# Chunked linear attention: scores and keys by separate TensorE passes instead of one merged product

## The chip, the cores and the metric

The kernel runs on one core of a Trainium2 chip. A core has five engines with queues of their own: TensorE (matmuls, PE in the profile, its weight loads PEld), VectorE (DVE), ScalarE (ACT), GpSimd (POOL) and SyncE (SP, which only issues DMAs here). They are joined by semaphores. The metric is the time on the device of one execution, in microseconds, as the median of several runs.

## The reference

An AdaLN block on x of 8 x 2048 x 256: a layer norm with modulation, gated linear attention, a gate and a residual, then a second layer norm with a mixture of 8 experts (two chosen for each token), a gate and a residual. The change touches the attention alone:

```
q = elu(x @ Wq) + 1        # 16 heads of 64
k = elu(x @ Wk) + 1
v = x @ Wv
a = sigmoid(x @ Wa + ba + 2.0)            # one decay for each head and token
def step(carry, inp):                     # along the 2048 tokens
    S = at[..., None, None] * S + kt[..., :, None] * vt[..., None, :]
    z = at[..., None] * z + kt
    num = einsum('bhk,bhkv->bhv', qt, S)
    den = einsum('bhk,bhk->bh', qt, z) + eps
    return (S, z), num / den[..., None]
out = out @ Wo
```

## The kernel before

The tokens go through in 32 groups of 512 (GT), and the recurrence along them is cut into chunks of 64 (CK), eight to a group (NCK). The heads are taken two at a time, 8 pairs (PAIRS) to a group. A **step** is one pair of one group, so there are 256 steps, with three more at the start in which only the early stages run. All engines walk through the same steps (`attention_steps`), the first and last groups unrolled, the ones between in a loop. The stages of a pair are spread over the steps: in step u TensorE makes K and Q for the pair three ahead (`project`, L594 to L596), applies the state to the queries of the pair one ahead (L741), makes the chunks' own state updates for the pair two ahead (L755), adds the masked scores times V for the pair one ahead (L766), transposes the output of the present pair (L782), does one or two large jobs of a fixed table (V, output projection, decays, the next group's transposes), and last comes the block that is changed (L803 to L822), for the pair three ahead. It waits for K and Q of its pair (`k_ready`, `q_ready`), for the readers of its PSUM tile (`kd_ready`, `p_ready`) and, except in the first step of a group, for `oT_hi_ready`, since L782 writes the same bank.

**The changed block.** K and Q of a pair lie transposed in SBUF (`qk_sb`): head 0 on partitions 0 to 63, head 1 on 64 to 127, 512 tokens along. The block makes two things from them. The scores of each chunk, S = K Q^T of 64 x 64 (tile `S`), which VectorE multiplies by a decay mask into `p_sb` (L980). And the keys turned to have tokens on the partitions (tile `KTR`), which ScalarE copies with a decay factor into `kd_sb` (L554, eight copies), the weights' partner in L755. Both are in `bank_scores`, one PSUM bank for each head, KTR in the first half of a bank and S in the second. `place(hd, ch)` says on which half of the partitions and in which column block t a chunk lands: head 0 in order, head 1 one chunk further back, so that its chunk 0 lands last, beside chunk 7.

Before, the two are one product. An identity of 64 x 64 (`eye`) lies in `qk_sb` ahead of Q, and the moving operand is a view with a stride that takes the identity and one chunk of Q, 2 x 64 columns (`eye_q`); the stationary operand is that chunk of K. So 16 products of 64 x 64 weights and 128 columns make both. Consecutive products lie on different quarters of TensorE's array of 128 x 128: the head gives the rows, `place` the columns. A product of fp32 operands is two records in the profile. GpSimd copies the identity to its place at the start (L413), and TensorE waits for it once (`eye_ready`).

The profile writes a product as out<-moving,stationary, with the weights' rows*columns, then the output's partitions x columns. A weight load has a record of its own (PEld).

Of the kernel before, what the change touches and what calls it, by code (L numbers as in the profile page):

```python
# [39 lines left out]
CH = 128  # L40
CK = 64
SLICE = CH // 4
NCH = 4
GT = CH * NCH
NCK = GT // CK
# [10 lines left out]
def after(eng, sem, count):  # L56

    if isinstance(count, int) and count <= 0:
        return
    eng.wait_ge(sem, count)  # L60


def exists(T):

    return not isinstance(T, int) or 0 <= T < NG
# [7 lines left out]
def unit(T, u, ahead):  # L73

    Tn, p = (T, u + ahead) if u + ahead < PAIRS else (T + 1, u + ahead - PAIRS)
    return Tn, p, Tn * PAIRS + p
# [49 lines left out]
def adaln_block(nc, x, Wq, Wk, Wv, Wo, Wa, ba, gate_W, gate_b, expert_W, expert_b, c, wmod, out):  # L126
    tokens = x.rearrange("b (g c p) d -> (b g) p c d", p=CH, c=NCH)
    out_tokens = out.rearrange("b (g c p) d -> (b g) p c d", p=CH, c=NCH)
    x1_dram = nc.dram_tensor("x1_dram", [NG, CH, NCH, D], F32, kind="Internal").ap()
    rows_dram = nc.dram_tensor("rows_dram", [2, 2, PAIRS, 2, GT], F32, kind="Internal").ap()  # L130
    gates_dram = nc.dram_tensor("gates_dram", [2, BATCH, D], F32, kind="Internal").ap()

    with ExitStack() as keep:
        mod = keep.enter_context(nc.sbuf_tensor("mod", [128, 4, KT, BATCH], F32))
        ident = keep.enter_context(nc.sbuf_tensor("ident", [128, 128], F32))
        def psum(name, shape):
            return keep.enter_context(nc.psum_tensor(name, shape, F32))

        single = [psum(f"bank{i}", [128, 512]) for i in range(2)]
        bank = single + [psum(name, [128, 2, 512]) for name in ("bank_scores", "bank_dense", "bank_nums")]  # L140
        attention_phase(nc, tokens, Wq, Wk, Wv, Wo, Wa, ba, c, wmod, x1_dram, gates_dram, rows_dram, mod, ident, bank)
        expert_phase(nc, x1_dram, gates_dram, gate_W, gate_b, expert_W, expert_b, out_tokens, mod, ident, bank)


def attention_phase(nc, tokens, Wq, Wk, Wv, Wo, Wa, ba, c, wmod, x1_dram, gates_dram, rows_dram, mod, ident, bank):
    with ExitStack() as ctx:
        def sb(name, shape, dt=F32):
            return ctx.enter_context(nc.sbuf_tensor(name, shape, dt))

        def sem(name):  # L150
            return ctx.enter_context(nc.semaphore(name))
# [11 lines left out]
        eye8 = sb("eye8", [128, NCK, CK])  # L163
# [7 lines left out]
        x_res = sb("x_res", [128, NCH, D])  # L171
# [18 lines left out]
        oT_lo = sb("oT_lo", [128, PT, GT], F32R)  # L190
        oT32 = sb("oT32", [128, GT])

        qk_sb = sb("qk_sb", [128, CK + 2 * GT])
        eye, q_sb, k_sb = qk_sb[:, 0:CK], qk_sb[:, CK:CK + GT], qk_sb[:, CK + GT:CK + 2 * GT]
        qs_sb = sb("qs_sb", [128, 2, GT])
        decay = sb("decay", [128, 2, NCH, CK])
        p_sb = sb("p_sb", [128, 2, 2, NCH, CK])
# [12 lines left out]
        Q, K, SCORES, EXTRA, NUM = bank[0][:, :], bank[1][:, :], *bank[2:]  # L210
        U_ODD, U_EVEN = EXTRA[:, 0, :], EXTRA[:, 1, :]
        KTR, S = SCORES[:, :, 0:GT // 2], SCORES[:, :, GT // 2:GT]
        HT = [K, SCORES[:, 1, :]]
        MODS, GATES = [NUM[:, 1, :], SCORES[:, 0, :]], NUM[:, 0, :]
        KTR_S = SCORES[:, :, :].rearrange("p h (x t i) -> p h x t i", x=2, t=NCH)
        U = [(U_EVEN, U_ODD)[ch % 2][:, ch // 2 * VW:(ch // 2 + 1) * VW] for ch in range(NCK)]
        def o_bank(u):

# [6 lines left out]
        consts_ready = sem("consts_ready"); ones_ready = sem("ones_ready"); fills = sem("fills")  # L225
# [14 lines left out]
        decay_ready = sem("decay_ready"); qs_ready = sem("qs_ready")  # L240
        s_ps = sem("s_ps"); p_ready = sem("p_ready")
        kd_ready = sem("kd_ready")
        u_ps = sem("u_ps"); eye_ready = sem("eye_ready"); entry_cleared = sem("entry_cleared"); state_step = sem("state_step")
        inter_ps = sem("inter_ps"); num_ps = sem("num_ps"); den_step = sem("den_step"); o_ready = sem("o_ready")
        oT_ps = sem("oT_ps"); oT32_ready = sem("oT32_ready"); oT_hi_ready = sem("oT_hi_ready"); oT_lo_ready = sem("oT_lo_ready")

# [1 line left out]
        def wide(t, dims):  # L248
            return t.rearrange(f"p {dims} -> p ({dims})")

        v_flat = wide(v_sb[:, :, :, :], "c h v")
        p_flat = wide(p_sb[:, :, :, :, :], "a h t i")
        qk_flat, qs_flat, res_flat = qk_sb[:, CK:CK + 2 * GT], wide(qs_sb[:, :, :], "a n"), wide(x_res[:, :, :], "c d")
        wmod_part = [[p_flat[:, 0:3 * D], qk_flat[:, 0:3 * D]], [qs_flat[:, 0:3 * D], res_flat[:, 0:3 * D]]]
        W = KT * P_DIM
        WV, WK, WQ, WO0, WO1 = range(5)
# [17 lines left out]
        def place(hd, ch):  # L274

            m = (ch - hd) % NCK
            return m % 2, m // 2

        def v_col(p, hd):

            return p // 4 * 8 + hd * 4 + p % 4
# [99 lines left out]
        def _(pool):  # L381
            def reciprocal_deviation(T):
                pool.wait_ge(var_ready, T + 1)
                pool.tensor_tensor(rstd[:, :], var_eps[:, :], half_neg[:, :], ALU.pow).then_inc(rstd_ready, 1)
# [24 lines left out]
            for t, fill, pattern in ((eye8[:, :, :], 1.0, [[0, NCK], [-1, CK]]), (first[:, :], 1.0, [[-1, 1]]), (later[:, :], 0.0, [[-1, 1]])):  # L409
                pool.affine_select(out=t, in_=t, compare_op=ALU.not_equal, fill=fill, base=-CK, pattern=pattern,  # L410
                                   channel_multiplier=1).then_inc(consts_ready, 1)
            pool.wait_ge(consts_ready, 4)
            pool.tensor_copy(eye, eye8[:, 0, :]).then_inc(eye_ready, 1)  # L413
            reciprocal_deviation(0)
            ln_apply(0, range(NCH))

# [51 lines left out]
        def _(act):  # L468
# [3 lines left out]
            def split_weight(n):  # L472
                hi, _, raws = big_w[n]
                act.wait_ge(w_loaded[n], 16 * LOADS[n])
                for part, raw in kept(hi, raws):
                    ins = act.activation(part, raw, ACT.Copy)
                ins.then_inc(hi_split, 1)
# [39 lines left out]
            def step(T, place_in_batch, u):  # L517
                s = place_in_batch % 2
                n = T * PAIRS + u
                Ta, _, a = unit(T, u, 3)  # L520
                if exists(Ta):

# [39 lines left out]
        def _(pe):  # L562
# [3 lines left out]
            for kt in range(KT):  # L566
                mm = pe.transpose(K[:, kt * BATCH:(kt + 1) * BATCH], c_e[:, kt * 128:(kt + 1) * 128],
                                  ident[0:BATCH, 0:BATCH])
# [138 lines left out]
            def step(T, place_in_batch, u):  # L707
                s = place_in_batch % 2
                n = T * PAIRS + u
                Tc, pc, c = unit(T, u, 1)  # L710
                Tb, pb, b = unit(T, u, 2)
                Ta, pa, a = unit(T, u, 3)
                sa = s if u + 3 < PAIRS else 1 - s
                sc = s if u + 1 < PAIRS else 1 - s
                rows = [slice(i * CK, (i + 1) * CK) for i in range(2)]
# [15 lines left out]
                if exists(Tc):  # L731
# [5 lines left out]
                    for ch in range(NCK):  # L737
                        state = carry[:, sc, pc, :] if ch == 0 else s_mid[:, pc % 2, ch - 1, :]
                        query = slice(ch * CK, (ch + 1) * CK)
                        for hd in range(2):  # L740
                            mm = pe.matmul(NUM[rows[ch % 2], hd, ch // 2 * VW:(ch // 2 + 1) * VW], qs_sb[rows[hd], pc % 2, query],  # L741
                                           state[rows[hd], :], start=(ch < 2), stop=False)
                    mm.then_inc(inter_ps, 1)
                if exists(Tb):
# [7 lines left out]
                    for ch in range(NCK):  # L752
                        for hd in range(2):
                            half, t = place(hd, ch)
                            mm = pe.matmul(U[ch][rows[hd], :], kd_sb[rows[half], t, rows[hd]], v_sb[rows[half], t, v_col(pb, hd), :],  # L755
                                           start=True, stop=True)
                    mm.then_inc(u_ps, 1)
                if exists(Tc):
# [4 lines left out]
                    for ch in range(NCK):  # L763
                        for hd in range(2):
                            half, t = place(hd, ch)
                            mm = pe.matmul(NUM[rows[ch % 2], hd, ch // 2 * VW:(ch // 2 + 1) * VW], p_sb[rows[half], pc % 2, hd, t, :],  # L766
                                           v_sb[rows[half], t, v_col(pc, hd), :], start=False, stop=(ch >= NCK - 2))
# [32 lines left out]
                if exists(Ta):  # L800

                    if isinstance(Ta, int) and a == 0:
                        pe.wait_ge(mod_ready, 4)  # L803
                        pe.wait_ge(gates_step, 4)
                    pe.wait_ge(k_ready, a + 1)
                    pe.wait_ge(q_ready, a + 1)
                    after(pe, kd_ready, a)
                    after(pe, p_ready, a)
                    if u and exists(T):
                        pe.wait_ge(oT_hi_ready, n + 1)  # L810
                    if u == 0 and exists(T + 1):
                        pe.wait_ge(h32_ready, T * 2 + 4)
                    if isinstance(Ta, int) and a == 0:
                        pe.wait_ge(eye_ready, 1)
                    pe.sem_inc(inputs_seen)
                    for ch in range(NCK):
                        eye_q = qk_sb[:, 0:2 * (ch + 1) * CK].rearrange("p (x i) -> p x i", x=2)[:, :, 0:CK]
                        for hd in range(2):
                            half, t = place(hd, ch)
                            mm = pe.matmul(KTR_S[rows[half], hd, :, t, :], k_sb[rows[hd], ch * CK:(ch + 1) * CK], eye_q[rows[hd], :, :],  # L820
                                           start=True, stop=True)
                    mm.then_inc(s_ps, 1)  # L822

            attention_steps(pe, step)

        @block.vector
        def _(dve):
# [16 lines left out]
            def split_weight(n):  # L844
                hi, lo, raws = big_w[n]
                dve.wait_ge(hi_split, n + 1)
                for (low, raw), (high, _) in zip(kept(lo, raws), kept(hi, raws)):
                    ins = dve.tensor_tensor(low, raw, high.bitcast(F32), ALU.subtract)
                ins.then_inc(lo_split, 1)
# [618 lines left out]
```

## Time and profile before

| | us |
|---|---|
| median of 3 runs | 3352.62 |
| the runs | 3346.16, 3352.62, 3356.04 |
| the profiled execution | 3356.36 |
| its span, first to last instruction | 3354.6 |
| TensorE busy | 3235.5 (96%) |
| VectorE, ScalarE, GpSimd busy | 2455.1, 1812.7, 1437.3 |

The attention phase ends near 2500 us; after it the experts' phase runs to the end. The profile gives starts and durations of single instructions. On TensorE a product's duration reaches from its start to a modelled end, and products overlap, so that the distance from start to start tells what one costs in a row of them. A timeline row joins neighbours of one line: its second number is the time from the first one's start to the last one's end, x its count.

### The profile page before, as it was taken

What the parts mean: (1) busy time and instruction counts of PE and PEld (TensorE: products, weight loads), DVE (VectorE), ACT (ScalarE), POOL (GpSimd) and SP (SyncE); (2) the same over time, 40 slices, a digit from 0 to 9 for tenths busy, and PEclk for the clock granted to TensorE, in tenths of its full rate; (3) what the DMA queues carried; (4) which work ended last, traced back from release to release, by engine and by line L of the source; (5) the groups of instructions that cost most, each with busy time, mean ns of one, the idle gap of its engine ahead of it and who ended that gap; (6) DMA issues with size and microseconds to landing.
All of it is one profiled execution on the core that took longest, in us unless ns stands there. A gap on an engine that the chain in (4) does not pass through costs nothing. (4 is left out here: it accounts for less than half of the span.)

```text
span 3354.6 us, 129353 instructions
## 1 busy us (share of the span) xinstructions
PE 3235.5 (96%) x51114; PEld 2748.1 (82%) x51114; DVE 2455.1 (73%) x6681; ACT 1812.7 (54%) x4492; POOL 1437.3 (43%) x1117
## 2 busy tenths in 40 slices
PE   7999999999999999999999999999987999999999
PEld 5888888888888888888888888888875888878887
DVE  6777777777777776777777777777756788878786
ACT  5666666666666666666666666666642322222321
POOL 4444445545544444455455444444431222222222
PEclk9999999999999999999999999999997999999999
DMA  4222222222222222222222322222212111111110
GB/s 150 75 76 78 80 79 79 79 73 75 83 90 79 76 79 76 79 79 77 74 75 81 92 78 77 78 77 79 72 43 83 46 44 39 51 39 39 51 39 26
DMA packets 158613, 238.74 MB, mean 71 GB/s; under 512 B 30216, under 2 KB 82488, under 8 KB 157752
## 3 DMA queue, kind: packets, MB, share of 16 engines
q1 hardware_dynamic: 158008, 230.33, 21.9%
q8 instruction: 421, 6.90, 0.9%
q14 instruction: 184, 1.51, 0.1%
HBM read 194.58 MB, written 35.67 MB: 69 GB/s over the span
## 5 line engine op out<-in xcount | busy, mean ns | idle before, releaser
L447 POOL TENSOR_TENSOR qs_sb<-lam_bc,qk_sb 128x512 f32<-128x512 f32 x256 | 534.0, 2086 | 1081.5 <-DVE qk_sb L945 980.1
L554 ACT ACTIVATE kd_sb<-bank_scores,decay 128x64 f32<-128x64 f32 x2048 | 446.2, 329 | 288.5 <-PE bank_scores L820 278.8
L928 DVE SCALAR_TENSOR_TENSOR s_mid<-s_mid,lam_bc,bank_dense 128x65 f32<-128x65 f32 x1536 | 433.4, 282 | 55.1 <-DVE s_mid L928 0.3
L455 POOL TENSOR_TENSOR oT_lo<-oT,oT_hi 128x512 fp32r<-128x512 f32 x256 | 327.4, 1279 | 79.4 <-ACT oT_hi L531 79.1
L513 ACT ACTIVATE qk_sb<-bank 128x512 f32<-128x512 f32 x512 | 316.7, 619 | 54.0 <-PE bank L596 36.4
L1140 POOL TENSOR_TENSOR acc<-acc,gb 128x512 f32<-128x512 f32 x64 | 82.9, 1296 | 583.3 <-DVE acc L1312 559.8
L515 ACT ACTIVATE qk_sb<-qk_sb 128x512 f32<-128x512 f32 x512 | 323.3, 631 | 16.2
L980 DVE TENSOR_TENSOR p_sb<-bank_scores,decay 128x512 f32<-128x512 f32 x256 | 176.5, 689 | 206.7 <-ACT kd_sb L554 204.8
L594 PE MATMUL bank<-wv_hi,h_hi 128*128 128x256 f32 x1024 | 307.3, 300 | 7.1 <-DVE qk_sb L943 4.0
L951 DVE TENSOR_TENSOR_SCAN decay<-a_bc,eye 128x512 f32<-128x512 f32 x256 | 310.9, 1214 | 2.4 <-DMA a_bc<-rows_dram 2.4
L1312 DVE SCALAR_TENSOR_TENSOR acc<-bank,comb,acc 128x256 f32<-128x256 f32 x512 | 229.9, 475 | 107.5 <-ACT acc L1180 97.0
L820 PE MATMUL bank_scores<-qk_sb 64*64 64x128 f32 x8192 | 287.0, 276 | 8.6 <-ACT oT_hi L531 4.3
L689 PE MATMUL bank<-wo_hi,oT_hi 128*128 128x256 f32 x1024 | 290.9, 284 | 1.6 <-DVE xo L858 0.8
L595 PE MATMUL bank<-wv_lo,h_hi 128*128 128x256 f32 x1024 | 288.3, 282 | 0.7 <-issue 0.7
L596 PE MATMUL bank<-wv_hi,h_lo 128*128 128x256 f32 x1024 | 289.0, 282 | 0.0
L691 PE MATMUL bank<-wo_hi,oT_lo 128*128 128x256 f32 x1024 | 288.3, 282 | 0.0
L690 PE MATMUL bank<-wo_lo,oT_hi 128*128 128x256 f32 x1024 | 288.1, 281 | 0.0
L945 DVE SCALAR_TENSOR_TENSOR qk_sb<-bank,qk_sb 128x512 f32<-128x512 f32 x256 | 176.6, 690 | 127.0 <-ACT qk_sb L515 126.0
L820 PEld LDWEIGHTS bank_scores<-qk_sb 64*64 64x64 f32 x8192 | 227.2, 133 | 49.2 <-issue 35.3
L1312 DVE SCALAR_TENSOR_TENSOR acc<-bank_scores,comb,acc 128x256 f32<-128x256 f32 x512 | 231.1, 476 | 44.1 <-PE bank_scores L1226 42.9
L530 ACT ACTIVATE oT<-bank_scores 128x512 f32<-128x512 f32 x224 | 134.0, 598 | 218.5 <-PE bank_scores L782 217.1
L594 PE MATMUL bank<-h_hi,wk_hi 128*128 128x512 f32 x512 | 227.9, 445 | 14.1 <-ACT oT_hi L531 10.0
(198 smaller groups left out, 8605.5 us busy)
## 6 DMA issues: line engine op xcount, KB each, us to landing
a_bc<-rows_dram SPq DMA_DIRECT2D x512, 128.0 KB, 3.0
lam_bc<-rows_dram SPq DMA_DIRECT2D x512, 128.0 KB
x_in<-in_L_attn_x_dram SPq DMA_DIRECT2D x32, 512.0 KB, 5.6
x_res<-in_L_attn_x_dram SPq DMA_DIRECT2D x32, 512.0 KB, 4.0
x_dram<-x_res SPq DMA_DIRECT2D x32, 512.0 KB, 2.9
x<-x_dram SPq DMA_DIRECT2D x32, 512.0 KB, 3.3
out_dram<-x SPq DMA_DIRECT2D x32, 512.0 KB, 2.9
ew_raw<-in_L_ffn_expert_W_dram SPq DMA_DIRECT2D x8, 256.0 KB, 5.5
```

Source lines behind the costliest of these rows:

```text
L447: pool.tensor_tensor(qs_sb[:, na, :], lam_bc[na][:, :], q_sb, ALU.mult).then_inc(qs_ready, 1)
L455: pool.tensor_tensor(oT_lo[:, u, :], oT32[:, :], oT_hi[:, u, :].bitcast(F32), ALU.subtract).then_inc(oT_lo_ready, 1)
L513: act.activation(t, x[:, :], ACT.Relu, scale=-1.0).then_inc(x_neg, 1)
L515: act.activation(t, t, ACT.Exp, scale=-1.0).then_inc(x_exp, 1)
L554: ins = act.activation(kd_sb[:, t, hd * DH:(hd + 1) * DH], KTR[:, hd, t * CK:(t + 1) * CK], ACT.Copy, scale=decay[:, hd, t, CK - 1:CK])
L594: pe.matmul(dst, s_hi, m_hi, start=(n == 0), stop=False)
L596: mm = pe.matmul(dst, s_lo, m_hi, start=False, stop=(n == last))
L689: pe.matmul(dst, oT_hi[:, pt, tok], wo_hi[:, pt, :], start=(pt == 0 and i == 0), stop=False)
L820: mm = pe.matmul(KTR_S[rows[half], hd, :, t, :], k_sb[rows[hd], ch * CK:(ch + 1) * CK], eye_q[rows[hd], :, :], start=True, stop=True)
L928: dve.scalar_tensor_tensor(dst, src, lam_bc[nb][:, (ch + 1) * CK - 1:(ch + 1) * CK], U[ch], ALU.mult, ALU.add).then_inc(state_step, 1)
L951: dve.tensor_tensor_scan(decay[:, :, :, :].rearrange("p h t i -> p (h t i)"), a_bc[na][:, :], eye8[:, :, :].rearrange("p c i -> p (c i)"), ...
L1312: dve.scalar_tensor_tensor(a, y[:, (k // 2) * D:(k // 2 + 1) * D], comb[s % 2][:, 2 * pair + i, e:e + 1], a, ALU.mult, ALU.add).then_inc(y ...
```

## The change

The block makes scores and keys apart.

- Scores: 16 products as before, but with the 64 columns of Q alone.
- Keys: where two neighbouring chunks lie on the 128 partitions of one column block, one transpose takes 64 rows and 128 tokens and writes all 128 partitions. There are seven of them, four for head 0 and three for head 1. In head 1's last column block chunks 7 and 0 meet, which aren't neighbours; these two stay products with an identity of 64 x 64, taken from `ident`.
- The last of the seven transposes tells the readers that the block is done. The identity in `qk_sb`, its copy on GpSimd and the wait for it are gone.

```
-        qk_sb = sb("qk_sb", [128, CK + 2 * GT])
-        eye, q_sb, k_sb = qk_sb[:, 0:CK], qk_sb[:, CK:CK + GT], qk_sb[:, CK + GT:CK + 2 * GT]
+        qk_sb = sb("qk_sb", [128, 2 * GT])
+        q_sb, k_sb = qk_sb[:, 0:GT], qk_sb[:, GT:2 * GT]
...
-            pool.wait_ge(consts_ready, 4)
-            pool.tensor_copy(eye, eye8[:, 0, :]).then_inc(eye_ready, 1)
...
-                    if isinstance(Ta, int) and a == 0:
-                        pe.wait_ge(eye_ready, 1)
                     pe.sem_inc(inputs_seen)
                     for ch in range(NCK):
-                        eye_q = qk_sb[:, 0:2 * (ch + 1) * CK].rearrange("p (x i) -> p x i", x=2)[:, :, 0:CK]
+                        tok = slice(ch * CK, (ch + 1) * CK)
                         for hd in range(2):
                             half, t = place(hd, ch)
-                            mm = pe.matmul(KTR_S[rows[half], hd, :, t, :], k_sb[rows[hd], ch * CK:(ch + 1) * CK], eye_q[rows[hd], :, :],
-                                           start=True, stop=True)
+                            pe.matmul(S[rows[half], hd, t * CK:(t + 1) * CK], k_sb[rows[hd], tok], q_sb[rows[hd], tok], start=True, stop=True)
+                    for ch in (NCK - 1, 0):
+                        half, t = place(1, ch)
+                        pe.matmul(KTR[rows[half], 1, t * CK:(t + 1) * CK], k_sb[rows[1], ch * CK:(ch + 1) * CK], ident[rows[1], rows[1]],
+                                  start=True, stop=True)
+                    for t in range(NCH):
+                        for hd in range(2 if t < NCH - 1 else 1):
+                            mm = pe.transpose(KTR[:, hd, t * CK:(t + 1) * CK], k_sb[rows[hd], t * CH + hd * CK:(t + 1) * CH + hd * CK],
+                                              ident[rows[hd], rows[hd]])
                     mm.then_inc(s_ps, 1)
```

On TensorE's queue, in a step whose large job is V: before, the block stands between V's last product and K's projection for the next pair. A name in brackets is a semaphore that is waited for; "64x2x64" is an output of 64 partitions and twice 64 columns.

```order
L596 MATMUL bank<-wv_hi,h_lo 128x256
L820 MATMUL bank_scores<-qk_sb 64x2x64 [waits p_ready,kd_ready,k_ready,q_ready]
L820 MATMUL bank_scores<-qk_sb 64x2x64 x15
L594 MATMUL bank<-h_hi,wk_hi 128x512 [waits v_ready,h_lo_ready]
L595 MATMUL bank<-h_lo,wk_hi 128x512
```

The same place now:

```order
L593 MATMUL bank<-wv_hi,h_lo 128x256
L815 MATMUL bank_scores<-qk_sb 64x64 [waits p_ready,kd_ready,k_ready,q_ready]
L815 MATMUL bank_scores<-qk_sb 64x64 x15
L818 MATMUL bank_scores<-ident,qk_sb 64x64 x2
L822 MATMUL bank_scores<-ident,qk_sb 128x64 x7
L591 MATMUL bank<-h_hi,wk_hi 128x512 [waits v_ready,h_lo_ready]
L592 MATMUL bank<-h_lo,wk_hi 128x512
```

Sixteen products have become 25 instructions in three kinds; the waits ahead and behind are the same, and nothing else on the queue has moved (its lines are numbered two or three lower).

On GpSimd's queue at the start, before:

```order
L410 AFFINE_SELECT chunk_later<-chunk_later 128x1
L413 COPY qk_sb<-eye 128x64 [waits consts_ready]
L384 TENSOR_TENSOR rstd<-var_eps,half_neg 128x4 [waits var_ready]
```

and now:

```order
L409 AFFINE_SELECT chunk_later<-chunk_later 128x1
L383 TENSOR_TENSOR rstd<-var_eps,half_neg 128x4 [waits var_ready]
```

The copy is gone.

## Rows read from the trace of the kernel before

**Rows 1.** Page, engines; windows: stretch, us, busy (instructions) by engine, clock, DMA.

```profile
PE 3235.5 (96%) x51114; PEld 2748.1 (82%) x51114; DVE 2455.1 (73%) x6681; ACT 1812.7 (54%) x4492; POOL 1437.3 (43%) x1117
...
100.00:2480.00 2380.00, 2331.25 (x43897) 2009.55 (x43888) 1732.91 (x4287) 1531.97 (x3954) 1174.48 (x828) 1.00 0.26 78
```

**Rows 2.** TensorE's waits from 100 to 2480 us: us in total, times, longest.

```profile
PE bank L594 <- DVE lam_row L902: 13.6, 24, 0.8
PE bank L594 <- ACT oT_hi L531: 8.9, 31, 0.3
...
PE bank_scores L820 <- issue: 0.5, 3, 0.2
```

**Rows 3.** Products by shape: busy us, mean ns; the third from the view of L820.

```profile
L820 PE MATMUL bank_scores<-qk_sb 64*64 64x128 f32 x8192 | 287.0, 276 | 8.6 <-ACT oT_hi L531 4.3 <-issue 0.5 <-ACT h L493 0.2
L755 PE MATMUL bank_dense<-v_sb,kd_sb 64*64 64x65 f32 x8192 | 173.3, 221 | 0.0
...
L820 PE MATMUL bank_scores<-qk_sb x8192: 266/269/473, 44.1 to 2486.2; 64*64 64x128 f32 x200
```

**Rows 4.** Timeline around one block: start, us to the last end, count.

```profile
1503.47 1.10 PE L820 MATMUL bank_scores<-qk_sb 64*64 64x128 f32 x32
...
1504.51 0.19 PEld L594 LDWEIGHTS bank<-h_hi,wk_hi 128*128 128x128 f32 x1 [0.17 <-issue]
```

**Rows 5.** The same block in three short windows, ending 0.11 us apart.

```profile
1503.47 0.34 PE L820 MATMUL bank_scores<-qk_sb 64*64 64x128 f32 x4
...
1503.47 0.45 PE L820 MATMUL bank_scores<-qk_sb 64*64 64x128 f32 x8
...
1503.47 0.56 PE L820 MATMUL bank_scores<-qk_sb 64*64 64x128 f32 x12
```

**Rows 6.** Timeline of the three blocks with 65 columns.

```profile
1499.80 0.27 PE L741 MATMUL bank_nums<-carry,qs_sb 64*64 64x65 f32 x2
...
1500.32 0.67 PE L755 MATMUL bank_dense<-v_sb,kd_sb 64*64 64x65 f32 x32
...
1500.78 0.67 PE L766 MATMUL bank_nums<-v_sb,p_sb 64*64 64x65 f32 x32
```

**Rows 7.** The transposes behind them: load, then two, three, four in growing windows.

```profile
1501.38 0.42 PEld L782 LDWEIGHTS bank_scores<-ident,o_sb 128*128 128x128 f32 x4
...
1501.38 0.44 PE L782 MATMUL bank_scores<-ident,o_sb 128*128 128x128 f32 x2
...
1501.38 0.55 PE L782 MATMUL bank_scores<-ident,o_sb 128*128 128x128 f32 x3
...
1501.38 0.66 PE L782 MATMUL bank_scores<-ident,o_sb 128*128 128x128 f32 x4
...
1501.55 0.49 PE L782 MATMUL bank_scores<-ident,o_sb 128*128 128x128 f32 x3
```

**Rows 8.** Timeline, experts' phase: from 128x128 to 128x32.

```profile
2560.85 0.40 PE L1226 MATMUL bank<-ew_hi,h_lo 128*128 128x512 f32 x1
2561.17 0.63 PEld L1244 LDWEIGHTS bank_dense<-gw,h 128*32 128x32 f32 x64 [0.36 <-issue]
```

**Rows 9.** Timeline, experts' phase: from 128 rows to 72.

```profile
2628.33 0.40 PE L1226 MATMUL bank<-ew_hi,h_lo 128*128 128x512 f32 x1
...
2628.34 0.67 PEld L1263 LDWEIGHTS bank_nums<-eb,combT 72*128 72x128 f32 x4
```

**Rows 10.** Weight loads of transposes by shape: busy us, mean ns.

```profile
L782 PEld LDWEIGHTS bank_scores<-ident,o_sb 128*128 128x128 f32 x896 | 94.5, 141 | 18.9 <-issue 3.6
L656 PEld LDWEIGHTS bank<-ident,a_cols 128*80 128x80 f32 x128 | 14.0, 118 | 1.6 <-issue 1.6
```

**Rows 11.** Timeline of the block's readers, and TensorE's next use of the keys.

```profile
1504.68 1.74 ACT L554 ACTIVATE kd_sb<-bank_scores,decay 128x64 f32<-128x64 f32 x8 [0.60 <-PE bank_scores L820]
...
1506.53 0.69 DVE L980 TENSOR_TENSOR p_sb<-bank_scores,decay 128x512 f32<-128x512 f32 x1
...
1508.02 0.69 PE L755 MATMUL bank_dense<-v_sb,kd_sb 64*64 64x65 f32 x32
```

More of the change, by code:

```diff
@@ L214, in attention_phase @@
         MODS, GATES = [NUM[:, 1, :], SCORES[:, 0, :]], NUM[:, 0, :]
-        KTR_S = SCORES[:, :, :].rearrange("p h (x t i) -> p h x t i", x=2, t=NCH)
         U = [(U_EVEN, U_ODD)[ch % 2][:, ch // 2 * VW:(ch // 2 + 1) * VW] for ch in range(NCK)]
@@ L242, in attention_phase @@
         kd_ready = sem("kd_ready")
-        u_ps = sem("u_ps"); eye_ready = sem("eye_ready"); entry_cleared = sem("entry_cleared"); state_step = sem("state_step")
+        u_ps = sem("u_ps"); entry_cleared = sem("entry_cleared"); state_step = sem("state_step")
         inter_ps = sem("inter_ps"); num_ps = sem("num_ps"); den_step = sem("den_step"); o_ready = sem("o_ready")
@@ L252, in attention_phase @@
         p_flat = wide(p_sb[:, :, :, :, :], "a h t i")
-        qk_flat, qs_flat, res_flat = qk_sb[:, CK:CK + 2 * GT], wide(qs_sb[:, :, :], "a n"), wide(x_res[:, :, :], "c d")
+        qk_flat, qs_flat, res_flat = qk_sb[:, 0:2 * GT], wide(qs_sb[:, :, :], "a n"), wide(x_res[:, :, :], "c d")
         wmod_part = [[p_flat[:, 0:3 * D], qk_flat[:, 0:3 * D]], [qs_flat[:, 0:3 * D], res_flat[:, 0:3 * D]]]
```

## The prediction

> **What bounds the kernel now.** Read the page's table of engines and the windows first [rows 1]: TensorE's matmuls are busy 3235.5 of 3354.6 us, and in the stretch from 100 to 2480 us, the attention phase, 2331.25 of 2380 us, at a granted clock of 1.00, which is the 2.4 GHz level. Busy time alone proves little, since the ends of matmuls are modelled, so read next what TensorE waited for in that stretch [rows 2]: 11 kinds of wait, from 13.6 us in 24 times down to 0.5, in 2380 us. No other engine holds it up. In that phase the time is the sum of what TensorE's queue takes, and what the change adds to or takes from that queue goes into the end nearly whole. The block that it rewrites (L820) runs once for each of 256 pairs of heads: 8192 matmul records are 32 a block, two to each of 16 products [rows 3]. It is nowhere after 2486 us, so the expert phase stays as it is.
>
> **How TensorE's queue is priced.** The durations in the grouped view overlap (276 ns each, but 35 ns of busy time for one), so I price by starts. One block of L820 [rows 4]: its first product starts at 1503.47, the next weight load (for K's projection, L594) at 1504.51. **The block takes 1.04 us.** Three windows that end 0.11 us apart show what it is made of [rows 5]: four products of 64x64, one on each quarter of the array, run together, and each four more lengthen the run from 0.34 to 0.45 to 0.56 us. So a round of four passes of 128 columns is 0.11 us; eight rounds are 0.88, the first has 0.02 more for a load that nothing hides, and 0.14 is left between the end of the last round (1504.37) and the load at 1504.51.
>
> The same with 65 columns [rows 6]: L741 starts at 1499.80, L755 at 1500.32, L766 at 1500.78. A block of 32 passes is 0.46 us, or 0.0575 a round, and L741, which like L820 comes behind products on the whole array, takes 0.52.
>
> Every change of the shape in which the array is cut costs a pause: the next weight load isn't done beside the last products. Behind L766 (64x64, the last round ends at 1500.78 + 8 x 0.0575 = 1501.24) the load of L782 (128x128) starts at 1501.38, 0.14 later [rows 6, 7]. Behind L1226 (128x128, started at 2560.85; a follower of its shape would come 0.23 behind, at 2561.08) the load of L1244 (128x32) starts 0.09 later [rows 8]. Behind a same-shaped product the load starts with the product before it (L1226 to L1263, 72 rows in a 128-row array, 0.01 us behind its start) [rows 9]. The new first weights then cost about 0.06 that nothing hides: L782's load at 1501.38, its second transpose at 1501.55, one round of 0.11 less [rows 7].
>
> **The change, part by part**, for one block.
> - Scores alone: 16 products of 64 columns in place of 128. The nearest row is L741's 0.52 for 65 columns behind whole-array products [rows 6]; with one column less, 0.51.
> - Two key products by the identity (the chunks that wrap round), 64x64, two passes each, both on the lower 64 rows and on different columns, so they run as a pair: two rounds of 0.0575, **0.115**. Same shape as the scores, so no pause.
> - Pause from 64x64 to 64 rows x 128 columns. No row shows this pair of shapes. Rows 6 to 8 bound it at 0.09 and 0.14 if a pause comes; rows 9 stand for none. I take 0.10, since at the end of a pair the last product starts nearly with the first, while four quarters start up to 0.05 apart. With 0.06 for the first weights: **0.16**.
> - Seven transposes, one record each, as L782's four are four records [rows 7]. L782 takes 0.11 each (0.44, 0.55, 0.66 us for two, three and four) with 128 moving columns and the whole array. The new ones move 64 columns. What sets the 0.11, the load of the weights or the moving columns? A transpose's load goes from 118 to 141 ns for 80 and 128 columns, about 0.48 ns a column, so it can run at 0.06 for 128; matmuls go from 221 to 276 ns for 65 and 128 columns, 0.87 ns a column, which is the 0.11 [rows 3, 10]. So the moving side binds and 64 columns should take 0.0575. Head 0 uses the upper 64 rows, head 1 the lower, with different banks; rows 5 show upper and lower halves at work together. Then four rounds do it: 4 x 0.0575 = **0.23**. One after the other it is 7 x 0.0575 = 0.40.
> - Pause at the end, to K's projection: 0.14 before, 0.10 now, since a single tile is last. **0.10**.
>
> Sum: 0.51 + 0.115 + 0.16 + 0.23 + 0.10 = 1.115 us against 1.04. **Each block takes 0.075 us more; 256 blocks, 19 us.** With both pauses at 0.09 it is 0.055 (14 us), with both at 0.14 0.155 (40 us).
>
> In other words: halving the scores' columns gives 0.52 - 0.11 x 8 = 0.42 back (0.88 to 0.46), and moving the keys by transposes costs 0.115 + 0.23 plus the extra pause of 0.16, which is more.
>
> The rest costs nothing. The copy of the identity on GpSimd goes from among its first instructions; TensorE's first block starts only at 44 us [rows 3]. The copies of the keys on ScalarE (L554) wait for the last product of the block, start at 1504.68 and take 1.74 us, to 1506.42; TensorE wants them at L755 at 1508.02 [rows 11]. 1.6 us of cover hide a start that is 0.1 later; were the cover gone, the same 0.1 would be added in each block. VectorE's masking (L980) follows them at 1506.53 and is wanted later still. The queue of waits on TensorE is as before but for one wait at the start. Against this some steps have waits that take up a later start (13.6 and 8.9 us over 55 steps [rows 2]); at 0.075 each they hide at most 4 us, which I leave out.
>
> Here a rule of the Trainium skill speaks against the change. By its page "TensorEngine Tiling (Array Packing)", Tiling Modes, Key Properties, another tiling mode drains TensorE where another tile of the same mode doesn't, and the page lists 64x128 and 64x64 as two modes. Rows 6 to 9 agree for other pairs of modes; without the drain the block would be 0.955, by the rule about 1.115. By its page "Perfetto Trace Analysis", Transposes, a logical transpose should be done as one and not as a product; the trace agrees that a transpose is one record and a product two [rows 3, 7], and the sum here goes the other way all the same.
>
> **The rivals.**
> - **One after the other** (slower still): the transposes of the two halves don't overlap. For it: all of them write all 128 partitions, and no row shows two tiles of 128 columns at once. Against: rows 5. Seven rounds in place of four: +0.17, so 0.245 a block, +63 us.
> - **A round of transposes stays at 0.11**, because the load or the mode binds and not the moving columns: 4 x 0.11 = 0.44, +0.21 more, so 0.285 a block, +73 us. Against it the slopes of rows 3 and 10. One after the other as well (7 x 0.11 = 0.77) it would be +157 us, the far bound, which I hold for very unlikely.
> - **No pause between the shapes** (the other side, faster): the array goes from quarters to halves as it goes from 128 to 72 rows in rows 9, because the columns of a half are only two quarters side by side. Then 0.16 goes and the block is 0.955, -0.085, -22 us. It decides at 0.085: where pause and first weights together cost less than that, the change gains. For it: no row has this pair. Against: L1226 to L1244 keeps all rows and cuts only columns, and pauses [rows 8].
> - **No pause, but one after the other**: 0.955 + 0.17 = 1.125, +22 us, as good as my forecast in time.
>
> **How the numbers follow.** Own sum 0.60; one after the other 0.18; 0.11 a round 0.07; no pause 0.12; no pause and in turn 0.03. The profiled execution took 3356.36 us; with 19 us it is 3375. It lies 4 us over the median of 3352.62, so against the median I forecast **3372 us**. The other cases against the median: 3416, 3426, 3331, 3375. The range leaves out "no pause" (0.12) and the far bound: from 3356, which is the low end of my sum less the 4 us of waits and the spread of the runs (3346 to 3356), to 3428. A measurement of this kernel can tell about 0.3%, 10 us, from no change. Faster by more: 0.12 of the no-pause case. Within: the low edge of my sum, 0.08. Slower: 0.80.
>
> **What would show it.** In the profile after: the start of the scores to the load of K's projection should be 1.1 us for 1.04; the 16 products 0.51; a gap of some 0.1 us before the first transpose's load; transposes in pairs of nearly the same start, 0.0575 apart. Transposes each 0.0575 apart mean one after the other; 0.11 apart, the load or mode binds; a first transpose load that starts with the last key product means no pause. ScalarE's wait for the block (278.8 us) should grow a little and cost nothing. Wrong would be: starts of other blocks that move too, a granted clock under 1.00 in the attention phase (transposes in place of products), or waits of TensorE that weren't there.

## The result

The changed kernel takes **3375.79 us** in the median of 4 runs (3375.30 to 3379.93), the kernel before 3353.09 (3346.16 to 3356.04). The ratio is 1.0074, with a 95% interval of 1.0062 to 1.0086 (the two medians alone give 1.0068): it is slower, by 22.7 us, under 1%. The profiled executions differ by 19.6 us in their spans, 3374.2 against 3354.6.

The page and the windows of the changed kernel, as [rows 1]:

```profile
span 3374.2 us, 134983 instructions
...
PE 3262.4 (97%) x53930; PEld 2785.5 (83%) x53930; DVE 2455.4 (73%) x6681; ACT 1814.8 (54%) x4492; POOL 1437.3 (43%) x1116
...
100.00:2500.00 2400.00, 2356.81 (x46646) 2044.85 (x46647) 1734.68 (x4290) 1534.48 (x3953) 1175.52 (x828) 1.00 0.25 78
```

TensorE has 2816 more matmul records, 11 for each of 256 blocks, and as many more loads. The other engines are as before, and the clock in the attention phase is again 1.00, so no part of the loss is the clock's. One block, the counterpart of [rows 4], in the timeline:

```profile
1517.30 0.69 PE L815 MATMUL bank_scores<-qk_sb 64*64 64x64 f32 x32
...
1517.82 0.29 PE L818 MATMUL bank_scores<-ident,qk_sb 64*64 64x64 f32 x4
1518.04 0.32 PEld L822 LDWEIGHTS bank_scores<-ident,qk_sb 64*128 64x128 f32 x7
1518.04 0.46 PE L822 MATMUL bank_scores<-ident,qk_sb 64*128 64x64 f32 x7
1518.43 0.19 PEld L591 LDWEIGHTS bank<-h_hi,wk_hi 128*128 128x128 f32 x1
```

L815 are the scores, L818 the two key products, L822 the transposes. From the first score to the load of K's projection it is 1.13 us where it was 1.04: 0.52 for the scores, 0.22 from the first key product to the first transpose's load, 0.39 from there to the end. The same block in growing windows, as [rows 5] and [rows 7]:

```profile
1518.04 0.28 PE L822 MATMUL bank_scores<-ident,qk_sb 64*128 64x64 f32 x2
1518.04 0.34 PE L822 MATMUL bank_scores<-ident,qk_sb 64*128 64x64 f32 x4
1518.04 0.40 PE L822 MATMUL bank_scores<-ident,qk_sb 64*128 64x64 f32 x6
```

Two more transposes lengthen it by 0.06 us: they run in pairs. Over all 256 blocks the median is 1.130 us against 1.033, by the starts in the trace to the nanosecond; that is 0.097 more. TensorE's waits, as [rows 2]:

```profile
PE bank L591 <- DVE lam_row L904: 11.8, 24, 0.8
PE bank_nums L763 <- issue: 8.9, 8, 1.6
PE bank L591 <- ACT oT_hi L528: 5.7, 29, 0.2
```

Those for `lam_row` and `oT_hi` fell by 1.8 and 3.2 us. A longer block takes up what TensorE would have waited in the few steps where another engine sets the time. So 256 x 0.097 - 5.0 = 19.8 us, against 19.6 measured between the spans. The rows named "issue" add up to 19.3 us here and 17.5 before, 1.8 more, which leaves the sum 2 us too high. Each kernel has one trace, and the kernel before varies by 12 us in 15 runs (3347.9 to 3359.7), so that no such sum can be trusted to less than some us.

### The profile page after: what moved, and what is told of

Read it like the earlier page. It is cut to its first block and busy times, and to the rows that moved or that the text cites. A ratio compares the mean times of both kernels' runs of the same rounds, so it can differ in the third digit from the quotient of the medians.

```text
span 3374.2 us, 134983 instructions
## 1 busy us (share of the span) xinstructions
PE 3262.4 (97%) x53930; PEld 2785.5 (83%) x53930; DVE 2455.4 (73%) x6681; ACT 1814.8 (54%) x4492; POOL 1437.3 (43%) x1116
## 5 line engine op out<-in xcount | busy, mean ns | idle before, releaser
L551 ACT ACTIVATE kd_sb<-bank_scores,decay 128x64 f32<-128x64 f32 x2048 | 446.2, 328 | 304.9 <-PE bank_scores L822 294.6
L947 DVE SCALAR_TENSOR_TENSOR qk_sb<-bank,qk_sb 128x512 f32<-128x512 f32 x256 | 176.7, 690 | 132.3 <-ACT qk_sb L512 130.6
L945 DVE SCALAR_TENSOR_TENSOR qk_sb<-bank,qk_sb 128x512 f32<-128x512 f32 x256 | 175.9, 687 | 61.7 <-ACT qk_sb L512 59.9
L591 PE MATMUL bank<-h_hi,wq_hi 128*128 128x512 f32 x512 | 204.4, 399 | 13.7 <-DVE lam_row L904 13.5
```

Source lines behind the costliest of these rows:

```text
L551: ins = act.activation(kd_sb[:, t, hd * DH:(hd + 1) * DH], KTR[:, hd, t * CK:(t + 1) * CK], ACT.Copy, scale=decay[:, hd, t, CK - 1:CK])
L591: pe.matmul(dst, s_hi, m_hi, start=(n == 0), stop=False)
```

## The experiments

My theory had three parts: TensorE's queue sets the time; a round of work that fills the array costs what its longer side (load or moving columns) takes; and each change between shapes of the array costs a pause and a first load that nothing hides. Each experiment changes one of these. Lengths of blocks are medians over 256, from the first product's start to the load of K's projection; times are medians, ratios are to the kernel before on the same chip. The experiments used three chips, on which the kernel before took 3353.1, 3350.1 (products of 128 columns, head by head, wrap products twice) and 3352.4 us (output in halves). In the experiments the lengths of the blocks came within 0.012 us of their forecasts but for head by head; four of the times missed theirs by 12 to 45 us, and that of head by head by 30. Where I add up below what makes a time, the waits and "issue" are read from the trace of that same run: it is an account afterwards, not a forecast.

| kernel | block, us | forecast | time, us | ratio (95%) |
|---|---|---|---|---|
| before | 1.033 | | 3353.1 | |
| changed | 1.130 | 1.115 | 3375.8 | 1.0074 (1.0062 to 1.0086) |
| all products | 1.090 | 1.09 | 3378.6 | 1.0078 (1.0063 to 1.0094) |
| products of 128 columns | 1.772 | 1.76 | 3489.6 | 1.0414 (1.0383 to 1.0444) |
| transposes split | 1.272 | 1.28 | 3405.1 | 1.0158 (1.0143 to 1.0174) |
| head by head | 1.130 | 1.25 to 1.31 | 3375.2 | 1.0073 (1.0050 to 1.0096) |
| wrap products twice | 1.246 | 1.246 | 3390.3 | 1.0117 (1.0088 to 1.0146) |
| transposes first | 1.127 | 1.13 | 3373.6 | 1.0062 (1.0046 to 1.0077) |
| ring of keys | 1.016 | 1.012 | 3349.6 | 0.9991 (0.9982 to 1.0000) |
| output in halves, with the ring | | | 3360.0 | 1.0022 (1.0012 to 1.0031) |

### One pause more: the transposes split

```
+                    for t in range(2):
+                        for hd in range(2 if t < NCH - 1 else 1):
+                            mm = pe.transpose(KTR[:, hd, t * CK:(t + 1) * CK], ...)
                     for ch in range(NCK):            # the scores
...
-                    for t in range(NCH):
+                    for t in range(2, NCH):
```

> The same work as in the changed kernel, with four of the seven transposes ahead of the scores and three behind, so that the array changes shape once more in each block. My theory: one more pause of 0.09 us and one more first load of 0.06, 0.15 a block, 38 us less what some steps hide, so 3376 + 35 = 3411. Rival, a change of shape costs nothing of its own and the gap ahead of the transposes is something else (the end of the block's queue, a wait): as the changed kernel, 3376.

```profile
1530.67 0.34 PE L813 MATMUL bank_scores<-ident,qk_sb 64*128 64x64 f32 x4
1530.93 0.56 PEld L819 LDWEIGHTS bank_scores<-qk_sb 64*64 64x64 f32 x32
...
1531.68 0.33 PE L826 MATMUL bank_scores<-ident,qk_sb 64*128 64x64 f32 x3
1531.94 0.19 PEld L591 LDWEIGHTS bank<-h_hi,wk_hi 128*128 128x128 f32 x1
```

In the timeline the four transposes (L813) start at 1530.67, and the load of the scores comes at 1530.93. By the starts in the trace (medians over all blocks) that load is 0.151 us behind the start of the last of the four; a round of 0.06 of that is work, and 0.09 is pause. With some 0.05 for the first load that nothing hides (in the changed kernel the second pair of transposes starts 0.112 behind the first, the next ones 0.06) it is about the 0.142 that the block grew. The block is 1.272 us against 1.130, by the same instructions in another order. The time is 3405.1, 29 us more, 6 less than expected: the waits for `oT_hi` and `lam_row` had 17.5 us to give in the changed kernel, and here only 5.7 are left. With 4.3 more at "issue" (idle time that is told of below) the sum is 256 x 0.142 - 11.8 + 4.3 = 28.9 us; the spans of the profiled executions, from which the waits come, differ by 24.4, the medians by 29.3. The pause has its price, and the rival without one is out.

### The place doesn't matter: all transposes first

```
+                    for t in range(NCH): ... mm = pe.transpose(...)     # all seven, ahead of the scores
                     for ch in range(NCK): ...
                     for ch in (NCK - 1, 0): ...
-                    for t in range(NCH): ... mm = pe.transpose(...)
```

> The same work as in the changed kernel, all seven transposes ahead of the scores, the two products by the identity last. As many changes of shape as in the changed kernel, in other places. My theory: 3376, within 5 us. Rival, the place matters (the first transposes wait for less, or the readers get the block's end at another time): off by more than 10 us.

3373.57 us, 2 us from the changed kernel; its own runs (3371.8 to 3379.8) take in the changed kernel's median. As many changes of shape, the same time; that they stand at the end and the readers wait for the last of them plays no part that can be seen.

### No third shape: all products

```
-                    for ch in (NCK - 1, 0):
+                    for ch in range(NCK):
+                        for hd in range(2):
+                            half, t = place(hd, ch)
+                            mm = pe.matmul(KTR[rows[half], hd, t * CK:(t + 1) * CK], k_sb[rows[hd], ch * CK:(ch + 1) * CK],
+                                           ident[rows[hd], rows[hd]], start=True, stop=True)
...
-                    for t in range(NCH): ... mm = pe.transpose(...)
```

> The scores as in the changed kernel, the keys as 16 products of 64x64 by the identity; no transposes and no third shape of the array. My theory (TensorE's queue is priced by rounds of 0.058 us and by pauses between shapes): 16 rounds of four passes, 0.93 us, with 0.05 at the start and 0.15 at the end make a block of 1.09 us against 1.033 before and 1.129 in the changed kernel, so about 14 us slower than before, 3366. Rival 1, the whole loss of the changed kernel comes from the transposes and their pause: without them as before, 3353. Rival 2, the loss comes from the number of instructions: here 64 passes and loads each where the changed kernel has 43, so slower than it, over 3385.

The block came out at 1.090 us, as forecast, 0.057 more than before: 16 rounds of 0.058 cost more than 8 of 0.109, so merging alone was worth that much. The time didn't: 3378.6, where 3366 was expected, and the same as the changed kernel's although its blocks are 0.04 shorter. Neither rival explains it. What does is the rows "issue" of the waits (stretch 100 to 2530):

```profile
PE bank_nums L763 <- issue: 9.4, 11, 1.5
PE bank L591 <- issue: 8.7, 6, 5.0
PE bank L591 <- ACT oT_hi L528: 7.2, 31, 0.2
```

"issue" is idle time in which TensorE waited for nothing that the profile shows. Added over its rows it is 17.5 us before, 19.3 in the changed kernel, 26.5 here. By the sum: 256 x 0.057 = 14.6, 4.0 less by the waits for `lam_row` and `oT_hi`, 9.0 more by "issue", 19.6 us; the spans differ by 21.0. Such a stop can stand in the midst of a block and come back at the same place of the program. Here is one in both passes of the loop, 936.4 us apart:

```profile
708.23 0.44 PE L819 MATMUL bank_scores<-ident,qk_sb 64*64 64x64 f32 x16
708.91 0.46 PE L819 MATMUL bank_scores<-ident,qk_sb 64*64 64x64 f32 x16 [0.24 <-issue]
...
1644.64 0.44 PE L819 MATMUL bank_scores<-ident,qk_sb 64*64 64x64 f32 x16
1645.33 0.46 PE L819 MATMUL bank_scores<-ident,qk_sb 64*64 64x64 f32 x16 [0.24 <-issue]
```

Sixteen records, 0.24 us of idle array, sixteen records, in the same step of the loop's body both times (the two blocks are 96 blocks apart). No semaphore stands between these records, and the place in the instruction stream plays a part. It isn't all of it: compared record by record over the two passes, 10 places of this kernel have a stop in both (neighbouring starts of one line over 0.1 us beyond the distance that 95% of that line keep to) and 10 in one pass alone; before there are 3 and 4, in the changed kernel 4 and 4. This kernel has the longest stream of the ten (485 instruction transfers on the page for 421 before). That the supply of instructions is the cause is argued, not shown; no run here changes it by itself.

### What sets a round: products of 128 columns

```
-                            mm = pe.transpose(KTR[:, hd, t * CK:(t + 1) * CK], k_sb[rows[hd], ...], ident[rows[hd], rows[hd]])
+                            mm = pe.matmul(KTR[:, hd, t * CK:(t + 1) * CK], k_sb[rows[hd], ...], ident[rows[hd], rows[hd]],
+                                           start=True, stop=True)
```

> The seven transposes as plain products of the same 64 rows and 128 columns by the identity, two passes each. My theory: a load of 128 columns for a plain fp32 pass takes twice that of a transpose, 0.11 us, so the load and not the 64 moving columns sets a round; eight rounds of 0.11, 0.88 us, in place of four of 0.06: 0.63 a block, 160 us, so about 3535. Rival, the moving columns set the round here too: eight rounds of 0.06, 0.24 more, 3435.

```profile
1584.13 1.10 PE L822 MATMUL bank_scores<-ident,qk_sb 64*128 64x64 f32 x14
1585.16 0.19 PEld L591 LDWEIGHTS bank<-h_hi,wk_hi 128*128 128x128 f32 x1
...
L822 PEld LDWEIGHTS bank_scores<-ident,qk_sb 64*128 64x128 f32 x3584 | 246.8, 187 | 17.3
```

Fourteen passes take 1.03 us where seven transposes take 0.39. The moving columns are the same 64; the load has changed, from 138 ns (the changed kernel's L822) to 187 ns on average. A plain product may differ from a transpose in more than that, so compare the scores too: they are plain passes with 64 moving columns, their loads of 64 columns take 134 ns, and a round takes 0.058. Both ways the load is about 0.05 us longer here and the round as well. So the load sets the round here, at 0.11, and the block is 1.772, 0.64 more, as expected. The time is 3489.6, and not 3535: of 164 us more in the blocks the spans show 112. The waits that could give way did: those for `lam_row` and `oT_hi` (17.5 us) are gone, and of "issue" 5.4 are left of 19.3. That is 31 us, and 21 are left. Most of them are in the way of counting, since idle time is counted from modelled ends, behind the real ones. From start to start, the blocks grew by 154.5 us in all and not by 164 (those of the changed kernel hold more waits and stops), 15.8 went ahead of Q's projection, where the waits for `lam_row` were, and 9.2 inside the products of L763; some 17 are left, in pieces of 3 us and less.

### Who runs with whom: head by head

```
-                    for t in range(NCH):
-                        for hd in range(2 if t < NCH - 1 else 1):
+                    for hd in range(2):
+                        for t in range(NCH - hd):
```

> The same seven transposes, the four of head 0 first and then the three of head 1, so that neighbours in the queue are on the same rows. My theory: the pairs of the changed kernel work at the same time because they are neighbours on different rows; in this order only the last of head 0 and the first of head 1 can, so six rounds of 0.0615 in place of four, 0.12 to 0.18 more, 31 to 46 us, 3405 to 3422. Rival, TensorE finds the other rows' transposes further down its queue: as the changed kernel, 3376.

```profile
1514.71 0.28 PE L822 MATMUL bank_scores<-ident,qk_sb 64*128 64x64 f32 x2
1514.71 0.35 PE L822 MATMUL bank_scores<-ident,qk_sb 64*128 64x64 f32 x4
1514.71 0.41 PE L822 MATMUL bank_scores<-ident,qk_sb 64*128 64x64 f32 x6
```

My theory fell. With head 0's four ahead of head 1's three the growing windows read as in the changed kernel, two more for each 0.06, and the block is 1.130. TensorE takes the other rows' transposes from further down its queue. The trace shows it: the last of the seven in the queue (head 1's third) is the one whose record carries the update of `s_ps`, and in 255 of 256 blocks it starts sixth, with another transpose starting behind it; in the changed kernel it starts last in all. That also rules out that any two neighbours pair, whatever their rows. That they run in pairs stands; that they must be neighbours for it doesn't. Whether the update could come before the one behind has ended, no run here shows.

### The price of the two key products: done twice

```
-                    for ch in (NCK - 1, 0):
+                    for ch in (NCK - 1, 0, NCK - 1, 0):
```

> The changed kernel with its two products by the identity done twice. My theory: two rounds of 0.058 more, 0.117 a block, 29 us less what some steps hide, 3403. Rival, the two overlap with what is around them and their price is near nothing: 3376 to 3383.

The block is 1.246, 0.116 more, as forecast for two rounds. The time is 3390.3, 14.5 us more than the changed kernel's and not 27. The blocks add 256 x 0.116 = 29.7; the waits for `lam_row` fell from 11.8 to 8.0 and those for `oT_hi` from 5.7 to none, 9.5; "issue" fell from 19.3 to 13.2. That leaves 14.1, and the spans differ by 15.1. The rival without a price for them is out by the block.

### Without them: the ring of keys

```
-        qk_sb = sb("qk_sb", [128, 2 * GT])
+        qk_sb = sb("qk_sb", [128, 2 * GT + CK])
+        k_ring = qk_sb[:, GT:2 * GT + CK]
...
+                    pool.wait_ge(k_ready, a + 1)
+                    pool.tensor_copy(k_ring[:, GT:GT + CK], k_sb[:, 0:CK]).then_inc(ring_ready, 1)
...
-                    for ch in (NCK - 1, 0): ...                            # the two key products
                     for t in range(NCH):
-                        for hd in range(2 if t < NCH - 1 else 1):
+                        for hd in range(2):                                # from k_ring in place of k_sb
```

> The two products by the identity are gone: the keys get 64 more columns, which GpSimd fills with a copy of chunk 0, so that chunks 7 and 0 of head 1 are neighbours and an eighth transpose takes them, in the round in which head 0's last was alone. My theory: two rounds of 0.058 go, the block is 1.129 - 0.117 = 1.012 us against 1.033 before; 3376 - 29 = 3347, some 5 us faster than before. Rival, GpSimd's copy comes late in some steps and TensorE waits for it: slower than the changed kernel in those steps, 3360 or more, with a new wait for GpSimd in the list.

```profile
1495.90 0.69 PE L819 MATMUL bank_scores<-qk_sb 64*64 64x64 f32 x32
1496.52 0.32 PEld L822 LDWEIGHTS bank_scores<-ident,qk_sb 64*128 64x128 f32 x8
...
1496.91 0.19 PEld L594 LDWEIGHTS bank<-h_hi,wk_hi 128*128 128x128 f32 x1
```

1.01 us, and 1.016 in the median. That is 0.114 less than the changed kernel's, the two rounds alone, so the eighth transpose costs nothing beside the seventh. GpSimd's copy takes 0.24 us and TensorE never waits for it. 3349.64 us in 11 runs against 3353.11: a ratio of 0.9991, whose interval reaches to 1.0000. It undoes the change's loss. It has the lowest time of the ten, by about 3 us, which can hardly be told from none.

### The same by halves for the output

```
                         for t in range(NCH):
+                            if u:
+                                for r in range(2):
+                                    mm = pe.transpose(SCORES[:, r, t * CK:(t + 1) * CK], o_sb[rows[r], t, :], ident[rows[r], rows[r]])
```

Here ScalarE's two copies read the two banks and put the halves back in order.

> The kernel with 64 more columns of keys, and in it the transposes of the output too by halves of the rows: in seven of eight steps eight transposes of 64 rows and 128 columns into two banks in place of four of 128 rows into one. My theory: four rounds of 0.0615 for four of 0.109, 0.19 less, and one more change of shape on the way to the next job, 0.09 and 0.06: 0.04 less in each of 224 steps, 9 us, so 3350 - 9 = 3341. Rival 1, ScalarE's two copies with the broken-up pattern take longer and hold TensorE up: 3350 or more. Rival 2, with the first load and the pause dearer in this place nothing is left: 3350.

```profile
1505.63 0.46 PE L790 MATMUL bank_scores<-ident,o_sb 64*128 64x64 f32 x8
1506.03 0.39 PE L598 MATMUL bank<-wv_hi,h_hi 128*128 128x256 f32 x1
...
1506.25 0.28 PE L599 MATMUL bank<-wv_lo,h_hi 128*128 128x256 f32 x1
```

Nothing was gained, and 3360.0 us is 10 more than the ring of keys alone. From the first transpose to V's second product it is 0.62 us; before, from 1501.38 [rows 7] to V's second product at 1502.00, it was 0.62 too. Rival 2 holds: the transposes save 0.19, and the pause and V's first load take it back. My price for the load, 0.06, was that of a transpose; a load of 128 plain columns costs more, as the products of 128 columns showed. The rest shows only in the profiled executions: the rows of "issue" add up to 31.0 us here and to 12.1 with the ring alone, less 3.4 by the wait for `lam_row`: 15.5, and the spans differ by 14.7. But the execution profiled here was the slowest of 12 (3367.1, of 3353.6 to 3367.1), so that the 10 us of the medians come from "issue" is likely and not shown. ScalarE's copies, at 599 and 593 ns, aren't longer.

## The prediction, point by point

- **TensorE's queue sets the time**: right. In seven of eight experiments the block's length, the waits that can give way and "issue" add up to the difference of the spans within 5 us. The prediction knew the second of these (4 us left out; 5.0 measured) and not the third.
- **Scores, 0.51**: 0.52. **Two key products, 0.115, with the pause, 0.215**: 0.22. Doubled they cost 0.116.
- **The pause between 64x64 and 64x128, with the first load, 0.16**, a bound from other pairs of shapes: it comes, and one more costs 0.142. Rows 9, where the shape stays that of the whole array, were rightly not taken for it. The Trainium skill's "TensorEngine Tiling (Array Packing)", Tiling Modes, Key Properties, says that a change of mode drains TensorE; the trace agrees for this pair too: the first transpose's load starts 0.147 us behind the last key product's start, 0.09 more than a round of 0.058.
- **Seven transposes in four rounds of 0.0575**: 0.06 a round. That the moving columns and not the load bind was right as far as it goes; for plain products of 128 columns it is the other way round. The reason that I gave for the pairs, rows 5, was sound as far as it went, and the picture of neighbours in the queue behind it, which the experiment's expectation spelled out, was wrong.
- **Last pause, 0.10**: transposes, first load and pause together 0.39, as forecast.
- **Sum, 1.115 for a block, 19 us**: 1.130, and 19.6 between the spans, 22.7 between the medians. The 0.015 are 0.01 in the scores and 0.005 in the key products. That 19 and 19.6 are so close is luck in part: a block grew by 0.097 and not by 0.075, since the sum is 0.015 short and the block before is 1.033 in the median and not 1.04; so the blocks alone make 25 us, and the 5.0 us of waits that the sum left out took that back. The time, 3375.8, lies 4 over the forecast of 3372, inside the range. The line behind the sum is written wrongly: 0.42 is 8 x 0.11 less 0.46, and by that line the change costs 0.505 - 0.42 = 0.085 a block, where the sum has 0.075.
- **Cover of the readers**: right. ScalarE's copies start 0.16 us behind the load of K's projection, as before (0.17), and TensorE waits neither for them nor for VectorE's masking. ScalarE's wait for the block grew from 278.8 to 294.6 us, as foreseen at no cost.
- **The rivals**: one after the other, 0.11 a round and no pause are all excluded by the rows above, for transposes. That the readers or the start matter is excluded by the transposes in first place.

## What to carry to other kernels

Price TensorE's queue by starts, in rounds of what runs at once, and count the changes of the array's shape: each cost about 0.14 us here (pause and first load), more than two rounds of 64 columns. A cheaper operation in another shape must save more than the pauses it brings, in each block. Where TensorE seems saturated, look for the waits that a longer block will take up and for stops at "issue", whose sum in the one trace of each version lay up to 19 us apart, more than a gain of 0.3%.

## What the runs showed of the hardware that was not expected

- Transposes on the upper and lower 64 rows run in pairs although four of one head stand ahead of three of the other in the queue (0.28, 0.34 and 0.40 us for two, four and six in the changed kernel, 0.28, 0.35 and 0.41 head by head). TensorE starts them out of the queue's order: the last in the queue starts sixth of seven in 255 of 256 blocks.
- A change of the array's shape leaves 0.09 us between the end of the last round and the next load, for 64x64 to 64x128 (0.147 from start to load, a round of 0.058) and for 64x128 to 64x64 (0.151, a round of 0.06) alike.
- A fp32 transpose's load of 128 columns is recorded with 138 ns, a plain fp32 product's of the same rows and columns with 187, and rounds are 0.06 and 0.11 us.
- Idle stops of TensorE with no semaphore behind them lie inside a run of like instructions (0.24 us after 16 records), and about half of their places have one in both passes of the loop (10 of 20 with all products, 4 of 8 in the changed kernel); their sum was 12 to 31 us in these kernels at nearly the same length of the phase, and 5 in the one whose blocks are longest.
